# Moving the values to four units behind the scores, the output product to nine, and reordering SyncE's queue in a cross-attention kernel

## What is computed

```
q = x @ Wq.T                              # (2, 2048, 640), 20 heads of 32
k, v       = text @ Wk.T,  text @ Wv.T    # 77 keys
k_ip, v_ip = ip @ Wk_ip.T, ip @ Wv_ip.T   # 77 more keys
out = softmax(q k^T / sqrt(32)) v + softmax(q k_ip^T / sqrt(32)) v_ip
y   = out @ Wo.T + bo + x
```

## Time and profile before

| | us |
|---|---|
| Median of the runs (lowest, highest) | 594.93 (592.18, 595.71) |
| The profiled execution's own time | 592.31 |
| Its span, first to last instruction | 590.2 |
| Busy: TensorE matmuls | 530.5 |
| Busy: VectorE | 400.9 |
| Busy: ScalarE | 386.2 |
| Busy: GpSimd | 309.9 |
| Mean granted TensorE clock, share of full | 0.983 |

### The profile page before, as it was taken

The page is one execution under the profiler, slowest core; times in us unless marked ns, Lnnn a source line. Parts: engine busy times, 40 slices in busy tenths (PEclk is TensorE's granted clock), DMA queues, the critical chain, the costliest instruction groups (busy, mean ns, idle before and its releaser), DMA issues.

```text
span 590.2 us, 15176 instructions
## 1 busy us (share of the span) xinstructions
PE 530.5 (90%) x4994; PEld 450.9 (76%) x4994; DVE 400.9 (68%) x655; ACT 386.2 (65%) x1714; POOL 309.9 (52%) x343
## 2 busy tenths in 40 slices
PE   8999577998898999899999999899999898979887
PEld 8998455777787788787778778788778777768776
DVE  0026567777776787777787777787777777686741
ACT  0235765686776777777778687778687777776730
POOL 1033446366554666574756556574756674754450
PEclk9999888899998999999999999999999999999999
DMA  8990265767576776767676867777766867656664
GB/s 299 413 376 23 81 214 171 218 213 239 182 235 199 229 228 207 249 210 237 226 249 202 252 212 240 221 234 220 234 228 213 255 199 239 206 195 209 204 211 150
DMA packets 87006, 130.14 MB, mean 220 GB/s; under 512 B 9792, under 2 KB 71872, under 8 KB 86720
## 3 DMA queue, kind: packets, MB, share of 16 engines
q1 hardware_dynamic: 86976, 129.75, 67.4%
HBM read 77.29 MB, written 52.43 MB: 220 GB/s over the span
## 4 chain that ended last, share of the span: by engine, by line
DMA 38%; SPq 28%; PE 16%; issue 7%; ACT 6%; DVE 3%; POOL 1%; DVEq 0%; POOLq 0%; ACTq 0%
DMA bounce_d<-turned 35%; SPq L288 18%; SPq L269 5%; SPq L276 5%; PE s_ps L768 3%; ACT probs L408 3%; PE q_ps L632 3%; PE pv_ps L768 2%; PE x_ps L632 2%; PE s_ps L657 2%; DVE row_neg L534 1%; DMA p_main<-bounce_d 1%; PE rest_ps L768 1%; DMA stage<-wk_in 1%; DVE wo_lo L526 1%
## 5 line engine op out<-in xcount | busy, mean ns | idle before, releaser
L345 POOL TENSOR_TENSOR probs<-probs,row_inv 128x616 f32<-128x616 f32 (+1 forms) x160 | 165.3, 1054 | 211.0 <-DVE row_inv L565 210.9
L408 ACT ACTIVATE probs<-s_ps,row_neg 128x77 f32<-128x77 f32 x640 | 197.6, 335 | 112.9 <-DVE row_neg L534 112.9
L534 DVE TENSOR_REDUCE row_neg<-s_ps 128x8 f32<-128x616 f32 x160 | 120.5, 795 | 84.4 <-PE s_ps L657 84.4
L408 ACT ACTIVATION_READ_ACCUMULATOR probs<-s_ps,row_neg 128x1 f32 x640 | 138.1, 216 | 0.0
L553 DVE STREAM_TRANSPOSE turned<-probs 128x512 f32<-128x512 f32 x160 | 103.7, 685 | 1.7 <-POOL probs L345 1.6
L632 PE MATMUL q_ps<-x_hi,wq_hi 128*128 128x256 f32 x400 | 90.5, 325 | 0.0
L560 DVE TENSOR_REDUCE row_sum<-probs 128x8 f32<-128x616 f32 x80 | 63.6, 795 | 39.4 <-ACT probs L415 39.4
L678 PE MATMUL pv_ps<-p_main,v 128*32 128x256 f32 x640 | 52.1, 397 | 29.7 <-DMA p_main<-bounce_d 28.5
L632 PE MATMUL q_ps<-x_hi,wq_lo 128*128 128x256 f32 x400 | 75.1, 287 | 0.0
L632 PE MATMUL q_ps<-x_lo,wq_hi 128*128 128x256 f32 x400 | 74.4, 284 | 0.0
L336 POOL TENSOR_TENSOR x_lo<-x_raw,x_hi 128x1280 fp32r<-128x1280 f32 x16 | 48.9, 3055 | 44.5 <-ACT x_hi L426 44.5
(11 more groups left out here) (72 smaller groups left out, 739.4 us busy)
## 6 DMA issues: line engine op xcount, KB each, us to landing
bounce_d<-turned SPq DMA_DIRECT2D x80, 512.0 KB, 3.2
p_main<-bounce_d SPq DMA_DIRECT2D x320, 128.0 KB, 2.8
x_raw<-x_in SPq DMA_DIRECT2D x16, 640.0 KB, 5.1
res<-x_in SPq DMA_DIRECT2D x75, 128.0 KB, 2.6
y_out<-res SPq DMA_DIRECT2D x75, 128.0 KB, 2.3
stage<-wk_in SPq DMA_DIRECT2D x6, 640.0 KB, 8.1
stage<-wv_in SPq DMA_DIRECT2D x6, 640.0 KB, 10.5
wq_raw<-wq_in SPq DMA_DIRECT2D x1, 1600.0 KB, 10.4
```

The costliest lines, as they stand in the source:

```text
L345: nc.gpsimd.tensor_tensor(rows[:, :, keys], rows[:, :, keys], row_inv[:, u.slot, :, br].unsqueeze(2) .broadcast_to([P, GROUP * SUB, size]) ...
L408: done = nc.scalar.activation(rows[:, cols], s_ps[:, j, cols], ACT.Exp, bias=row_neg[:, j, i:i + 1], accum_out=row_sum[:, j, i:i + 1])
L534: nc.vector.tensor_reduce(row_neg[:, heads_of(half)], by_row(s_ps[:, heads_of(half), 0:SUB * BLK]), AXIS.X, ALU.max, negate=True).then_inc ...
```

## The change

Lags: `VALUE_LAG` from 3 to 4, `OUT_LAG` from 8 to 9. `p_rest` gets five places instead of two. The semaphore of the write is split in two, one for each place of `turned`. SyncE issues the write of u-1 first in a unit, then the reads of u-2, residual load and store. ScalarE copies the rest of u-2 first in a unit. TensorE transposes the rest of u-1 ahead of the output product. The counts of the waits and the ends of all streams follow from the lags.

```diff
-OUT_LAG = 8
-VALUE_LAG = 3
+OUT_LAG = 9
+VALUE_LAG = 4
...
-        p_rest = sbuf("p_rest", [P, 2, N])
+        p_rest = sbuf("p_rest", [P, GROUPS, N])
...
-        bounced = sem("bounced")
+        bounced = [sem(f"bounced{n}") for n in range(2)]
...
 # SyncE
             def load_turned(u):
-                wait(sp, bounced, u.number(DMA, DMA))
+                wait(sp, bounced[u.slot], u.uses_of_slot(DMA))
...
             def emit(u):
-                ahead, old, new = u.tile_plus(2), u.plus(-OUT_LAG - 2), u.plus(GROUPS - OUT_LAG - 3)
+                ahead, old, new = u.tile_plus(2), u.plus(-OUT_LAG - 1), u.plus(GROUPS - OUT_LAG - 2)
+                if u.plus(-1).exists():
+                    bounce(u.plus(-1))
                 if u.plus(-2).exists():
                     load_turned(u.plus(-2))
                 if new.exists() and not (new.fixed and new.number() >= LAST.number()):
                     load_residual(new)
                 if old.exists():
                     store(old)
-                if u.plus(-1).exists():
-                    bounce(u.plus(-1))
...
             load_residual(LAST.plus(-1))
-            store(LAST.plus(-5))
-            load_turned(final.plus(-1))
-            store(LAST.plus(-4))
             bounce(final)
-            store(LAST.plus(-3))
-            load_turned(final)
-            store(LAST.plus(-2))
+            for u in (final.plus(-1), final):
+                load_turned(u)
+            for m in range(-5, -1):
+                store(LAST.plus(m))
 # ScalarE
             def emit(u):
                 ahead, nxt = u.tile_plus(2), u.plus(Q_AHEAD)
                 chunk = u.plus(-OUT_LAG)
+                if u.plus(-2).exists():
+                    keep_rest(u.plus(-2))
                 exp_direct(u)
                 exp(u)
...
-                if u.plus(-2).exists():
-                    keep_rest(u.plus(-2))
                 if chunk.exists():
                     add_bias(chunk)
...
             keep_rest(final.plus(-1))
+            add_bias(LAST.plus(-4))
+            attn_high(final.plus(-3))
             add_bias(LAST.plus(-3))
+            attn_high(final.plus(-2))
             add_bias(LAST.plus(-2))
-            attn_high(final.plus(-2))
 # VectorE
                 if part == 0:
-                    wait(dve, bounced, u.number(DMA, -DMA))
+                    wait(dve, bounced[u.slot], u.plus(-2).uses_of_slot(DMA))
...
-            attn_low(final.plus(-2))
             for part in range(BRANCHES):
                 turn(final, part)
+            for m in (-3, -2):
+                attn_low(final.plus(m))
 # TensorE
+                project_out(LAST.plus(-4))
+                weigh_values(final.plus(-3))
                 project_out(LAST.plus(-3))
+                weigh_values(final.plus(-2))
                 project_out(LAST.plus(-2))
-                weigh_values(final.plus(-2))
...
                 if u.plus(Q_AHEAD).exists():
                     project_q(u.plus(Q_AHEAD))
+                turn_rest(u.plus(-1))
                 if chunk.exists():
                     project_out(chunk)
-                turn_rest(u.plus(-1))
```

More of the change, by code:

```diff
@@ L281, in bounce @@
                 sp.dma_start(bounce_d[u.g].rearrange("p b n -> p (b n)"),
-                             turned[:, u.slot].rearrange("p b q k -> p (b q k)")).then_inc(bounced, DMA)
+                             turned[:, u.slot].rearrange("p b q k -> p (b q k)")).then_inc(bounced[u.slot], DMA)
             def load_turned(u):
-                wait(sp, bounced, u.number(DMA, DMA))
+                wait(sp, bounced[u.slot], u.uses_of_slot(DMA))
                 for b in range(BLOCKS):
@@ L389, in _ @@
             normalise_rest(LAST.plus(GROUPS - 1))
-            for m in (-4, -3, -2):
+            for m in range(-5, -1):
                 add_residual(LAST.plus(m))
@@ L419, in keep_rest @@
                 wait(act, rest_turned, u.number(1, 1))
-                nc.scalar.activation(p_rest[:, u.slot], rest_ps[:, 0:N], ACT.Copy).then_inc(rest_kept, 1)
+                nc.scalar.activation(p_rest[:, u.g], rest_ps[:, 0:N], ACT.Copy).then_inc(rest_kept, 1)
             def split_x(u):
@@ L680, in weigh_values @@
                                      start=True, stop=False, skip_group_check=True)
-                nc.tensor.matmul(pv_ps[:, 0:N], v[:, u.g, BATCHES + u.batch, :], p_rest[:, u.slot], start=False, stop=True,
+                nc.tensor.matmul(pv_ps[:, 0:N], v[:, u.g, BATCHES + u.batch, :], p_rest[:, u.g], start=False, stop=True,
                                  skip_group_check=True).then_inc(pv_ready, 1)
```

## The result

The changed kernel takes 547.61 us, the median of four runs (547.14 to 547.73), against 594.6 before: a ratio of 0.921 with a 95% interval of 0.918 to 0.924. The forecast was 551, with a range from 543 to 566. The profiled execution took 547.71 us, its span is 545.7.

The account below looks back on a forecast made before the run. Bounds: a 6.18 us loop over the rest's copy and, above it, SyncE's lap. Steady part -38.5, start -5, unit 78 -0.5, end +2.8: -41.2 from 592.31 gives 551 us; forecast range 545 to 556, over the cases 543 to 566.

Parts of the forecast that it names:

- steady, 70 units: Units from 108.00 to 554.89: 408.4 us forecast against 446.9, at a period of 5.76 us.
- start, six units: Six units before the first output product: VectorE's 5.4 us sets the period; 5 us gained, bounds 0 and 7.4.
- unit 78: The unit from 554.89 to 560.79 goes from 5.90 to about 5.4 us: -0.5.
- end: Behind the last scores, one more output product and one more values' product are left: +2.8 us.
- The two bounds: Per unit: 6.18 us by ScalarE's late copy of the rest and, above it, SyncE's lap, costing 14.3 us in all.
- the lap: One round of SyncE's queue: 3.2 us for a write to land plus 3.1 of issues, 6.3 us.
- The copy costs nothing at the head of the unit: ScalarE idles 1.80 us before its first exponential, so the rest's 0.44 us copy fits there free.
- The seams: TensorE's gaps between q product, transposes, output product and scores: 0.60 us after against 0.58 before, period 5.76.
- The cover of the reads: Last read lands at S+9.4, used at S+12.3 (S: start of a unit's scores): 2.9 us spare.
- the rival of late reads: Write and reads share DMA queues, reads land 3.2 us later, period 5.9: +10 us, 561; chance 0.14.
- The wait behind the split of x: Every fifth unit ScalarE's split delays the exponential, and the values' product waits for VectorE's low part: 14 x 0.4 = 5.6 us.
- the rival that the low level would take the whole gain of the start: TensorE's clock stays low through the first six units, which then gain nothing: 556 us; chance 0.10.

Follow-up runs that it names:

- x in two: Changed kernel with each x tile loaded in two transfers, groups 0 to 2 and groups 3 and 4, instead of one: 542.98 us, ratio 0.914.
- the split alone: Changed kernel with only ScalarE's split of x moved ahead of the bias copy, x tile still in one transfer: 545.18 us, ratio 0.918.
- the repeat: The changed kernel measured once more, unaltered, on one chip with two of the follow-up kernels: 546.36 us, ratio 0.918.

## Why the prediction was right

By its own parts, on the profiled executions, the change of each against the forecast:

| part | forecast | measured |
|---|---|---|
| steady, 70 units | -38.5 | 408.74 - 446.89 = -38.2 |
| start, six units | -5 | 32.50 - 41.32 = -8.8 |
| unit 78 | -0.5 | 5.12 - 5.90 = -0.8 |
| end | +2.8 | 33.11 - 29.41 = +3.7 |
| ahead of the units | 0 | 66.23 - 66.68 = -0.5 |
| span | -41.2 | 545.7 - 590.2 = -44.5 |

**The two bounds** were right. Undoing the copy's and the transposes' order brings 6.18 back; undoing SyncE's order brings the lap back; neither half alone gives more than about a fifth. The lap was 6.43 us in the mean, where I took 6.3.

**The copy costs nothing at the head of the unit**, right: S+0.48, ahead of an exponential that starts at S+1.70, as it did (1.71). The rows also show that I should have named what the transposes' place does: with the copy late it is ruin (767), with the copy early it is worth nothing (546.08 against 547.61). The 0.44 us belongs to the copy alone.

**The seams**: 216.17 to 216.38 is the 0.21 taken for product to scores; transposes to product took 0.14 instead of 0.27, and the product behind them 1.75 instead of 1.66. Period 5.73 for 5.76.

**The cover of the reads** was mis-sized in its term and in its price. I had the last read issued at S+6.6 and landing 2.8 later, by the medians before. Once write and reads stand in the queues together the four issues take 2.2 us in an ordinary unit, and 2.8 to 3.3 behind an x load, instead of 1.74, and the median read 3.5 to land: in an ordinary unit about S+10.2, 2 us of cover. Behind an x load it is 311.27 + 5.49 = 316.76, which is S+12.6 by a unit that began at 304.12, and the cover is gone. So the rival of late reads held, but only in units of group 0, in 9 of the 13 that stand behind an x load. And the price is not half of the lateness. A late unit between units in time pays all of it: the nine waited 5.7 us in all, and together they are 6.2 us longer than nine units of 5.73. Were each unit late, the product of unit u would wait for reads issued in u-2, and three periods would share it; this follows from the order, and no run shows it.

**The wait behind the split of x**, 14 x 0.4 = 5.6 us, came near the right sum for the wrong reason, and that is luck. The profile shows no wait of TensorE for the low part in units 10 to 77, where I had forecast one in every fifth. Where the split does show, the values' product waits for the copied rest, which now stands behind it on ScalarE: 0.16 us in unit 71, and in six units of the kernel with x in two. What the units of group 0 lost, 14 x 0.45 = 6.3 us, was the x load in front of the reads; the split cost the units of group 1 0.04 in the mean, since a unit that is already late hides it, and 0.18 once that was mended. Experiments tell the two apart: with x in two, group 0 falls to 5.73; with the split alone it stays at 6.08. These 6.3 us, 0.6 in group 1 and 1.1 in unit 9 are 2.4 more than I had put down, and the period of 5.73 instead of 5.76 gave 2.1 of it back.

**The start** gained more than my upper bound of 7.4. The bound left out that without a low part of the values VectorE's loop is shorter than 5.4 in the first of these units (units of 4.90 and 5.26), and TensorE ran ahead of VectorE, so that it pays back 1.14 us in unit 9 (6.87). The clock of the window is 0.84, as it was (0.83): it fell again, but beneath VectorE's loop it cost little. Unit 3 took 5.26 us at a granted 0.50. Unit 5 took 6.77 at 0.75 and the next 4.37, together 11.14, where the same two in the repeat, at 1.00, took 10.59. So the rival that the low level would take the whole gain of the start, which I gave 0.10, did not come. The Trainium skill ("TensorE: Matmul & The Clock Gate", Part 1) says that the low level is the default and that activity releases it. The trace agrees in that the window with the pauses was granted 0.84, and the steady part 1.00.

**The end** is 0.9 longer than forecast. TensorE waits for GpSimd's rest in each of the two last units, 1.0 us each, one of them in unit 78: without a product of q in front the transposes come too early. But with the transposes behind the product both waits are gone, and unit 78 and the end take 38.6 us together, against 38.2. So these waits are not what made the end longer; that stays open.

The median of the four runs equals the profiled one, as assumed when I gave the 2.6 us between them to late transfers; the spread of the runs fell from 3.5 to 0.6 us in this set, and was 5.3 us in the repeat, so this assumption is not shown.

## What to carry to other kernels

When two loops of nearly the same length hold a stage, list both and price each alone: here each half by itself gave nothing to 2%, both gave 8%. Look where a queue that waits for its own transfer could wait for something already done, and buy the unit of lag that this needs: the order without the lag cost 28%. Then look at the cover that is left by the worst unit, not by the median: one large load in front of small ones, whose landing the next stage waits for, undid it in most of the units behind such a load, and cutting the load in two, with the split that it had hidden moved too, gave 1% back.

## What the runs showed of the hardware that I had not expected

- A pause of some 2 us of TensorE in each unit costs more than its length, here 0.7 us a unit on top. In the kernel with the copy last, the same 59 or 60 matmuls of a unit took 6.95 us at a granted clock of 0.87 and 5.91 at 1.00, and the steady part was 609 us where 7.97 a unit would give 558.
- With the write just ahead of the reads SyncE's four issues take 2.2 us (2.8 to 3.3 behind an x load) instead of 1.74. In the kernel with SyncE's old order and all else changed, where the write has landed before they go out, they take 1.74 in the median again.
- Cutting one 640 KB load into 384 and 256 KB at two places left the DMA share of the steady part where it was (0.86, against 0.84) and took 0.45 us off every fifth unit, in the mean.
